# Down product of three tiles with row-scaled fp16 weight halves, on one Trainium2 core

## The reference, cut to what matters

```python
x = x + gnn(xn, edge_index, W, b) + mix(xn, Wq, bq, Wk, bk, Wv, bv, Wo, bo)
xq = act_fake_quant(layernorm(x), clip_x)          # integers times one scale
gate = xq @ weight_fake_quant(w_gate).T            # 352 columns
up   = xq @ weight_fake_quant(w_up).T
h = act_fake_quant(silu(gate) * up, clip_down)
x = x + h @ weight_fake_quant(w_down).T            # (1250, 352) @ (352, 1024)
```

## Time and profile before

| | us |
|---|---|
| timed runs | 746.82, 748.60, 748.89 |
| median | 748.6 |
| the profiled execution | 748.37 |
| its span | 746.6 |
| TensorE matmul busy | 708.0 (95%) |
| VectorE busy | 495.0 (66%) |
| GpSimd busy | 272.0 (36%) |
| ScalarE busy | 209.5 (28%) |
| down product's first matmul | at 720.08 |

### The profile page before, as it was taken

One profiled execution on the slowest core, in us unless ns is written; L12 is line 12 of the kernel. 1 busy time (PEld: TensorE's weight loads), 2 busy tenths in 40 slices (PEclk: granted clock), 3 DMA queues, 4 the chain that ended last, 5 costly groups with the idle time before them and its releaser, 6 DMA issues.

```text
span 746.6 us, 12015 instructions
## 1 busy us (share of the span) xinstructions
PE 708.0 (95%) x3772; PEld 361.7 (48%) x3772; DVE 495.0 (66%) x975; ACT 209.5 (28%) x346; POOL 272.0 (36%) x403
## 2 busy tenths in 40 slices
PE   4999999999999999999999999999999999995984
PEld 2455555555555554666644444444444444443651
DVE  7878887887666655656842213657777788756667
ACT  5133334643333244446212212500000000012350
POOL 5566677898666655540010000011111111110018
PEclk9999999999999999999999999999999999996988
DMA  9652422541000000003030300242222222001406
GB/s 343 216 134 65 100 48 65 172 168 57 0 0 0 0 2 1 2 0 113 1 113 0 113 0 0 88 118 71 68 64 62 60 59 70 28 6 31 82 26 249
DMA packets 52764, 52.18 MB, mean 70 GB/s; under 512 B 36482, under 2 KB 37514, under 8 KB 52720
## 3 DMA queue, kind: packets, MB, share of 16 engines
q1 hardware_dynamic: 52720, 51.61, 22.9%
HBM read 37.96 MB, written 5.12 MB: 58 GB/s over the span
## 4 chain that ended last, share of the span: by engine, by line
PE 68%; issue 13%; DVE 9%; POOL 4%; ACT 2%; DMA 2%; DVEq 1%; POOLq 0%; SPq 0%; ACTq 0%
PE bank L532 31%; PE bank L724 12%; PE bank L698 10%; PE bank L606 10%; POOL mem L491 2%; DVE mem L1014 2%; PE bank L517 2%; ACT mem L812 2%; PE bank L549 2%; DVE counts L1104 1%; DVE mem L1184 1%; DMA mem<-in_x 1%; PE bank L673 1%; DVE mem L1030 1%; DMA mem<-in_L_gnn_W 1%
## 5 line engine op out<-in xcount | busy, mean ns | idle before, releaser
L532 PE MATMUL bank<-mem 128*128 128x512 f16 x1440 | 327.6, 381 | 4.9 <-DVE mem L1030 1.7
L532 PEld LDWEIGHTS bank<-mem 128*128 (+1 forms) x1440 | 137.9, 98 | 158.5 <-issue 6.9
L443 POOL TENSOR_SCALAR hot_src<-iota_p,src_col 125x128 bf16<-125x128 bf16 x252 | 174.3, 706 | 14.1 <-issue 14.1
L1104 DVE TENSOR_TENSOR counts<-bank,counts 128x120 f32 x328 | 92.4, 282 | 49.1 <-issue 8.4
L606 PE MATMUL bank<-mem 128*128 128x512 f16 (+2 forms) x576 | 105.3, 339 | 0.8 <-DVE mem L1143 0.8
L724 PE MATMUL bank<-mem 128*128 128x512 f16 x480 | 105.4, 379 | 0.0
L698 PE MATMUL bank<-mem 128*128 128x512 f16 x400 | 88.0, 379 | 0.0
L606 PEld LDWEIGHTS bank<-mem 128*128 128x128 f16 (+1 forms) x576 | 55.2, 98 | 42.5 <-DVE mem L1143 1.4
L724 PEld LDWEIGHTS bank<-mem 128*128 128x128 f16 x480 | 47.0, 98 | 55.7
L832 ACT ACTIVATE src_gap<-iota_p,loT 125x128 bf16<-125x128 bf16 x84 | 33.7, 402 | 114.4 <-PE bank L517 105.8
L480 POOL TENSOR_TENSOR mem<-mem 128x1024 f32<-128x1024 f32 x10 | 23.5, 2348 | 114.4 <-DMA mem<-in_L_mix_bo 114.4
(11 more groups left out here) (148 smaller groups left out, 644.4 us busy)
## 6 DMA issues: line engine op xcount, KB each, us to landing
mem<-in_x SPq DMA_DIRECT2D x18, 512.0 KB, 3.8
out_x<-mem SPq DMA_DIRECT2D x9, 512.0 KB
mem<-in_L_mix_Wk SPq DMA_DIRECT2D x4, 1024.0 KB, 9.5
mem<-in_L_mix_Wv SPq DMA_DIRECT2D x4, 1024.0 KB, 8.6
mem<-in_L_mix_Wq SPq DMA_DIRECT2D x4, 1024.0 KB, 5.2
mem<-in_L_gnn_W SPq DMA_DIRECT2D x4, 1024.0 KB, 5.2
mem<-in_L_mix_Wo SPq DMA_DIRECT2D x2, 2048.0 KB, 7.9
mem<-in_L_ffn_w_down SPq DMA_DIRECT2D x4, 352.0 KB, 3.1
```

The source lines that it names most:

```text
L443: pool.tensor_scalar(hot_src[0:EC, i, c, :], iota_p[0:EC, :], src_col[0:EC, i, c:c + 1], None, ALU.is_equal).then_inc(S["hot_src_ready"], 1)
L532: last = pe.matmul(o[:, :], xT[:, a * K + k, bass.ds(t * P, P)], w16[i][:, k, b, :], start=(at == 0), stop=(at == len(parts) - 1))
L1104: dve.tensor_tensor(window, agg[i][:, k * WC:(k + 1) * WC], window, ALU.add).then_inc(S["adj_added"], 1)
```

## The change

- `hq`, `wdT` and the staging of the down weights become fp16 instead of bf16 (the integers are exact in both).
- `d_row` is scaled by `W_UP` = 256 when it is moved, and `s_d` by 1/256.
- GpSimd multiplies `wdT` by `d_row` into `y_t[b]`, f32, for the three blocks b, once `q_ready` has reached 6. ScalarE copies each to fp16 (`wd_half[0]`) after its silus of units 4, 5 and 6; GpSimd subtracts that from the f32 value into fp16 (`wd_half[1]`). The two halves together are the scaled weight.
- Tiles 7, 8 and 9 (`Y_SPLIT`) are multiplied with both halves, 6 matmuls for each half row instead of 3. VectorE then scales a bank by `s_d` and adds `x2` in one instruction, straight into `x2`.
- `Y_DVE` changes for the others: GpSimd adds whole rows for tiles 0 to 4 and columns 512 to 1024 of tile 5; VectorE adds columns 0 to 512 of tile 5 and all of tile 6.
- VectorE waits for all of `wd_half` before its first tile, TensorE before tile 7.
- SyncE's stores are written out one by one, each with the waits of its tile, in tile order.

```diff
-Y_DVE = [304] * (T - 1) + [560]
+Y_SPLIT = (7, 8, 9)
+Y_DVE = [0] * 5 + [HALF, D]
...
+        wd_half = [part(RAW + a * FB * D // 2, FB, D, dt=F16) for a in range(2)]
...
+            for t in range(T):
+                rows = LAST if t == T - 1 else P
+                if t in Y_SPLIT:
+                    sp.wait_ge(SC["y_moved"], 2 * t + 2)
+                else:
+                    if Y_DVE[t] > 0:
+                        sp.wait_ge(SC["y_dve"], sum(w > 0 for w in Y_DVE[:t + 1]))
+                    if Y_DVE[t] < D:
+                        sp.wait_ge(SC["y_pool"], t + 1)
+                sp.dma_start(out[P * t:P * t + rows, :], x2[0:rows, t, :]).then_inc(SC["stored"], 16)
...
+            pool.wait_ge(SC["d_row"], 2)
+            pool.wait_ge(SC["q_ready"], 6)
+            for b, n in enumerate(FR):
+                pool.tensor_tensor(y_t[b][0:n, :], wdT[0:n, b, :], d_row[0:n, :], ALU.mult).then_inc(SC["wd_scaled"], 1)
+            for b, n in enumerate(FR):
+                pool.wait_ge(SC["wd_hi"], b + 1)
+                pool.tensor_tensor(wd_half[1][0:n, b, :], y_t[b][0:n, :], wd_half[0][0:n, b, :],
+                                   ALU.subtract).then_inc(SC["wd_lo"], 1)
+
-            for t in range(T):
+            for t in range(len(Y_DVE) - 1):
                 s = slice(Y_DVE[t], D)
...
+                if t == Y_SPLIT[0]:
+                    pe.wait_ge(SC["wd_lo"], FB)
...
+                    weights = wd_half if t in Y_SPLIT else [wdT]
                     for b in range(FB):
                         r = FR[b]
-                        last = pe.matmul(y_bank[2 * (t % 4) + n][:, :], hq[0:r, b, t * P:(t + 1) * P],
-                                         wdT[0:r, b, n * HALF:(n + 1) * HALF], start=(b == 0), stop=(b == FB - 1))
+                        for w in weights:
+                            last = pe.matmul(y_bank[2 * (t % 4) + n][:, :], hq[0:r, b, t * P:(t + 1) * P],
+                                             w[0:r, b, n * HALF:(n + 1) * HALF], start=(b == 0 and w is weights[0]),
+                                             stop=(b == FB - 1 and w is weights[-1]))
...
+                if what == "u" and i in (4, 5, 6):
+                    b = i - 4
+                    act.wait_ge(SC["wd_scaled"], b + 1)
+                    act.activation(wd_half[0][0:FR[b], b, :], y_t[b][0:FR[b], :], ACT.Copy).then_inc(SC["wd_hi"], 1)
...
+            dve.wait_ge(SC["wd_lo"], FB)
             for t in range(T):
-                s = slice(0, Y_DVE[t])
-                if t >= 4:
-                    dve.wait_ge(SC["y_ready1"], t - 3)
+                if 4 <= t < Y_SPLIT[0]:
+                    dve.wait_ge(SC["y_pool"], t - 3)
...
+                    if t in Y_SPLIT:
+                        dve.scalar_tensor_tensor(x2[:, t, half], y_bank[2 * (t % 4) + n][:, :], s_d, x2[:, t, half], ALU.mult,
+                                                 ALU.add).then_inc(SC["y_moved"], 1)
```

More of the change, by code:

```diff
@@ L122, in gps_layer @@
         at += K * FF
-        wdT = part(at, FB, D, dt=BF16)
+        wdT = part(at, FB, D, dt=F16)
         at += FB * D // 2
@@ L138, in gps_layer @@
         hT = part(H0, FB, NP)
-        hq = part(H0 + FB * NP, FB, NP, dt=BF16)
+        hq = part(H0 + FB * NP, FB, NP, dt=F16)
         y_t = [part(H0 + FB * NP * 3 // 2 + i * D, D) for i in range(4)]
         assert FB * NP * 3 // 2 + 4 * D <= T * D
+        wd_half = [part(RAW + a * FB * D // 2, FB, D, dt=F16) for a in range(2)]
         x_half = part(EXTRA, 4, D, dt=F16).rearrange("p (i a) d -> p i a d", a=2)
@@ L160, in gps_layer @@
         raw16 = [part(XT + 2 * SLOT + T * P, D, dt=BF16), hot_dst_mem[:, :]]
+        raw_down = [part(XT + 2 * SLOT + T * P, D, dt=F16), hot_dst_mem[:, :].bitcast(F16)]
         hot_src = sb("hot_src", [P, 2, G, P], BF16)
@@ L198, in gps_layer @@
         SC = sems("clip_in", "c_step", "m_prev", "m_ready", "m_all", "exp", "silu_table", "h_max", "h_rs", "h_8", "hq_first", "d_row", "gus", "xn_columns", "affine", "q_ready", "qT_full",
-                  "qT_moved", "qT_in0", "qT_in1", "qT_in2", "qT_in3", "gate_full", "silu", "up_moved", "h_rounded", "hq", "y_full", "y_moved", "y_ready0", "y_ready1", "stored")
+                  "qT_moved", "qT_in0", "qT_in1", "qT_in2", "qT_in3", "gate_full", "silu", "up_moved", "h_rounded", "hq", "y_full", "y_moved", "y_dve", "y_pool", "wd_scaled", "wd_hi", "wd_lo", "stored")
         def over_tiles(tile):
@@ L371, in transpose_piece @@
                         sp.dma_start_transpose(wdT[:, :, (a + k) * P:(a + k + 1) * P],
-                                               raw16[i % 2][:, k * PITCH:(k + 1) * PITCH]).then_inc(SF[f"wT_in{i % 2}"], 16)
+                                               raw_down[i % 2][:, k * PITCH:(k + 1) * PITCH]).then_inc(SF[f"wT_in{i % 2}"], 16)
             load_piece(0)
@@ L490, in _ @@
                 pool.wait_ge(S["consts"], 3)
-                pool.tensor_tensor(x2[:, t, s], x2[:, t, s], y_t[t % 4][:, s], ALU.add).then_inc(SC["y_ready1"], 1)
+                pool.tensor_tensor(x2[:, t, s], x2[:, t, s], y_t[t % 4][:, s], ALU.add).then_inc(SC["y_pool"], 1)
         @block.tensor
@@ L916, in piece16 @@
                 if pieces[i][0] == "down":
-                    act.activation(raw16[i % 2][:, 0:2 * PITCH].rearrange("p (k i) -> p k i", i=PITCH)[:, :, 0:FF],
+                    act.activation(raw_down[i % 2][:, 0:2 * PITCH].rearrange("p (k i) -> p k i", i=PITCH)[:, :, 0:FF],
                                    raw8[i % 2][:, 0:2 * FF].rearrange("p (k i) -> p k i", i=FF),
@@ L928, in _ @@
             for j in range(2):
-                act.activation(d_row[:, j * HALF:(j + 1) * HALF], kv_acc[j][:, :], ACT.Copy).then_inc(SC["d_row"], 1)
+                act.activation(d_row[:, j * HALF:(j + 1) * HALF], kv_acc[j][:, :], ACT.Copy, scale=W_UP).then_inc(SC["d_row"], 1)
             act.activation(clip[:, 7:8], clip[:, 6:7], ACT.Silu).then_inc(SC["silu_table"], 1)
@@ L1403, in _ @@
             dve.tensor_tensor(rs_d, max_inv, clip[:, 7:8], ALU.mult).then_inc(SC["h_rs"], 1)
-            dve.tensor_tensor(s_d, m_col, clip[:, 5:6], ALU.mult)
+            dve.scalar_tensor_tensor(s_d, m_col, 1.0 / W_UP, clip[:, 5:6], ALU.mult, ALU.mult)
             dve.drain()
             dve.tensor_copy(hq[:, :, 0:P], h8[:, :, 0:P]).then_inc(SC["hq_first"], 1)
+            dve.wait_ge(SC["wd_lo"], FB)
             for t in range(T):
-                s = slice(0, Y_DVE[t])
-                if t >= 4:
-                    dve.wait_ge(SC["y_ready1"], t - 3)
+                if 4 <= t < Y_SPLIT[0]:
+                    dve.wait_ge(SC["y_pool"], t - 3)
                 for n in range(2):
@@ L1414, in _ @@
                     dve.wait_ge(SC["y_full"], 2 * t + n + 1)
[L1415 to L1418, removed]
+                    if t in Y_SPLIT:
+                        dve.scalar_tensor_tensor(x2[:, t, half], y_bank[2 * (t % 4) + n][:, :], s_d, x2[:, t, half], ALU.mult,
+                                                 ALU.add).then_inc(SC["y_moved"], 1)
+                    else:
+                        dve.scalar_tensor_tensor(y_t[t % 4][:, half], y_bank[2 * (t % 4) + n][:, :], s_d, d_row[:, half],
+                                                 ALU.mult, ALU.mult).then_inc(SC["y_moved"], 1)
+                if t not in Y_SPLIT and Y_DVE[t] > 0:
+                    s = slice(0, Y_DVE[t])
+                    dve.wait_ge(SC["y_moved"], 2 * t + 2)
+                    dve.tensor_tensor(x2[:, t, s], x2[:, t, s], y_t[t % 4][:, s], ALU.add).then_inc(SC["y_dve"], 1)
 _INS = ['x', 'src', 'dst', 'L0_gnn_W', 'L0_gnn_b', 'L0_mix_Wq', 'L0_mix_bq', 'L0_mix_Wk', 'L0_mix_bk', 'L0_mix_Wv',
```

## The result

The changed kernel takes 749.27 us (median of 22 runs, 747.66 to 750.24), the kernel before 748.43 us (22 runs, 746.82 to 748.98). The ratio is 1.0013, 95% interval 1.0007 to 1.0019: about 1.0 us slower, less than the 0.3% that I called measurable ahead. Measured again beside the experiments it was 748.87 us, ratio 1.0014 (1.0005 to 1.0022). Forecast: 749.6 us.

The account below looks back on a forecast made before the run. The prediction took GpSimd's residual adds in the down product, in turns with VectorE, to bound the kernel. 748.37 us plus 1.35 (gate and up products) minus 0.1 (last stage) gave 749.6 us, range 747.0 to 753.3.

Parts of the forecast that it names:

- What bounds the kernel before: Down product: GpSimd's residual adds one after another, 1.89 us a tile, lengthened by mutual exclusion with VectorE.
- Last stage, engines: Down product: GpSimd done at 738.2, TensorE at 740.1, VectorE last at 740.9, 2.1 us ahead of the old end.
- One sign: Expected in the profile after, last stage: GpSimd done 5 us before the end.
- Last stage, stores: End of down product: the queue of stores returns nearly the whole 2.1 us; stage -0.3 to +0.2 us, taken as -0.1.
- Gate and up products: GpSimd's multiplies and subtracts delay VectorE's casts and up instruction; TensorE stalls 1.35 us ahead of its unit 6.
- the price of GpSimd's instruction with 16-bit operands: Gate and up products: each 1024-column multiply or subtract taken at the f32 add's 2.348 us, not under 2.2.
- the 757 ns cast: Upper bound for GpSimd's 16-bit instruction: a cast of 128 columns, 4.7 ns a column, 4.9 us if all per column.
- The exclusion itself: VectorE and GpSimd share a port pair: an SBUF-only VectorE instruction and a GpSimd instruction wait for each other's whole length.
- Rival 1: Exclusion costs less: no stall in gate and up products, last stage -0.3 or -1.6; 746.8 to 748.1 us, chance 0.21.
- Rival 2: Gate and up products: GpSimd's mixed-format instructions slower, first subtract passes tile 8's tensor_scalar, 4.3 us stall; 752.6 or 753.3 us, chance 0.31.
- Rival 3: Last stage: the extra weight pass doesn't hide if the clock rises late, TensorE's end decides; 749.9 us, chance 0.04.
- The sum: Whole kernel: +1.35 us in gate and up products and -0.1 in the last stage, +1.25 us in all.

Follow-up runs that it names:

- half stores: Stores only columns 0 to 512 of each output tile: changed kernel so edited 746.13 us, ratio 0.9971; kernel before so edited 747.29 us, ratio 0.9992.
- one_pass: Changed kernel with tiles 7 to 9 multiplied by the high half of the scaled weight alone, 60 matmuls: 748.93 us, ratio 1.0010 to the kernel before.
- prep_only: Changed kernel's weight-half preparation kept but used by no tile; down product done as in the kernel before: 748.49 us, ratio 1.0004 to the kernel before.
- prep_late: Changed kernel with GpSimd's multiplies held until q_ready is 10, ScalarE's copies moved to units 6 to 8: 748.17 us, ratio 1.0000 to the kernel before.
- one_more_multiply: Changed kernel with one more 1024-column GpSimd multiply ahead of the three, into an unread buffer: 750.33 us, ratio 1.0027 to the kernel before.

## Why the prediction was right, point by point

- **What bounds the kernel before**: right, GpSimd's adds in turns with VectorE's. The kernel with half stores gained just 0.6 us, so the bytes did not bound it.
- **Last stage, engines.** The steps came out in kind: GpSimd starts tile 0 2.4 us behind TensorE instead of 3.6, because the clock stood; VectorE's two adds took 1.02 and 1.95 us by waiting (I had about 2.0 and 1.9); GpSimd was done at 737.72, 16.7 us after the first matmul (I had 18.1), and TensorE 17.1 us after it (I had 20.0). The low clock that I assumed, as in the earlier trace rows, is one of several that executions of this kernel show. Where it did come, in the change with half stores, GpSimd was done 18.1 us and VectorE 20.95 us after the first matmul (739.11, 741.93 and 720.98); I had 18.1 and 20.8. One sign was a slip: I wrote that GpSimd would be done 5 us before the end, which is its distance to the old last add; my own sum gives 8.2 to 8.7, and it is 8.7.
- **Last stage, stores**: right in mechanism. The queue behind GpSimd's last tiles gives the end. GpSimd's last add is followed by the end of the span after 8.6 to 8.7 us in both profiles of the change and in one_pass, while TensorE ends 17.1, 18.8 and 14.9 us behind its first matmul. I had the queue beginning with tile 5; it begins with tile 4. The size was a little low: the term was -0.3 to +0.2 us, I took -0.1, and at like clocks the stage is some 0.2 to 0.3 us longer than before. From the first matmul to the end of the span it is 26.5 us before, 25.4 and 26.0 in the two profiles of the change, but at different clocks. With the clock low for 3.4 us the change has 26.0; the old stage, in the kernel before with half stores, has GpSimd done 22.2 us behind the first matmul, and with the 3.4 to 3.6 us that follow it where stores are whole (prep_only, before) that makes an estimate of 25.7 to 25.8. With the clock low for 5 to 6 us, where GpSimd starts 3.6 us behind the first matmul in each, the old stage has 26.5 (before and prep_only); the change with half stores has GpSimd done after 18.1, and with 8.6 to 8.7 more that makes an estimate of 26.7 to 26.8. The old stage at a clock that never falls was not profiled.
- **Gate and up products**: right in mechanism, too dear: 1.35 us forecast, 0.28 us of pause and 0.43 us of stage in the trace (0.25 us in prep_only's). The step that failed is the price of GpSimd's instruction with 16-bit operands. I took the f32 add, 2.35 us, and excluded less than 2.2. (From above I had 4.7 ns a column out of the 757 ns cast; 757/128 is 5.9, and 4.7 only if a fixed start is taken off first. It bounded a rival and not the forecast.) Three multiplies back to back take 6.34 us in prep_late, 2.11 each. Three times 0.24 us is nearly all of the 0.8 us by which VectorE's tensor_scalar of tile 8 came early: 9.4 us behind the cast of tile 5 (692.94 to 702.33), where I had 10.2. So cast 8 slipped in ahead of the first subtract, and only cast 9 had to wait for it. The exclusion itself is as the rows of before showed it, and as the Trainium skill states it ("SBUF — State Buffer", section "Who interferes with whom"): the trace agrees, 3.12 us for two casts of 1.3, and 5.06 with one GpSimd instruction more.
- **The rivals.** Rival 1 (no exclusion) fell with the 1.86 us tensor_scalar and with one_more_multiply. Rival 2 (slower by mixed formats) fell with the same 2.11 us, but its place is real: with four multiplies the first subtract does go ahead of the tensor_scalar of tile 8. The price was 1.0 us and not 4.3, because TensorE had already lost 0.32 us, the second subtract was asked for at 707.2, behind both casts, and did not hold them up. Rival 3 fell with one_pass, where TensorE was done 3.9 us earlier and the end didn't move.
- **The sum.** +1.25 us forecast, +0.97 measured (0.5 to 1.4). That the two are so close is partly luck: the gate and up products were priced at least three times too high, the last stage 0.3 to 0.4 us too low, and what is left of the measured number I had not named. From the traces 0.25 to 0.43 us of it lies in the gate and up products and, by the estimates above, 0.2 to 0.3 us in the last stage; the remaining few tenths are not pinned to a row. Prep_late, with the preparation out of the way, is level with the kernel before (-0.7 to +0.7 us), and prep_only at +0.3 us (-0.4 to +1.0); both agree with these sizes.

## What to carry to other kernels

When an engine's chain is shortened at the end of a kernel, look at what the transfers behind it will do: results that become ready together wait in one queue of stores, and the last one waits for all of them; here the same work with its stores further apart was 1.0 us faster. The chain of waits of a profile doesn't show such a queue, the windows of DMA share do. And an idle GpSimd is not free: count its instructions against each tensor_scalar, cast and SBUF-only add of VectorE beside them, in the order in which they ask. Not against its reductions, though they read SBUF alone too: in the change one of 512 columns stands at 707.09 beside a subtract of GpSimd (706.93 to 709.06), and takes the same 0.69 us as in the kernel before at 700.35, where GpSimd does nothing.

## What the runs showed that I had not expected

- GpSimd's two-input instruction was quicker where an operand has 16 bits: 2.11 us each for f32 from f16 and f32, and 2.10 for f16 out, against 2.35 us for f32 alone, all with 1024 columns (prep_late's rows above, and the earlier trace rows). The operation differs too, multiply and subtract against add, and no run here tells the two apart.
- With several stores outstanding, SyncE's issue of the next becomes longer itself: 0.33 us for tiles 4 and 5 of the change, 1.23 us for its last one.
- TensorE's granted clock at the start of the same stage, after the same 1.8 us of idling, was low for none of it, for some 3.4 us or for some 6 us in different executions; in the second profile of the change it fell only at about 721.5, half a microsecond after the matmuls had begun again. It goes with part of the 2 us by which the runs of either kernel differ: of the 22 runs of the change, the five with a mean granted clock of 0.988 or more took 747.66 to 748.25 us, the other 17, at 0.986 or less, 748.31 to 750.24. That it is this stage's clock that makes the difference is my reading; between the two profiles of the change it accounts for 0.6 us.
